# Shared feed-forward of an attention and mixture-of-experts block in pairs of half-precision numbers

## What is computed

```python
# x: (8, 256, 512), ctx: (8, 256, 512); 16 heads of 16 in 256 channels, 512 positions
q = Wq @ layernorm(x) + bq ; k = Wk @ ctx + bk ; v = Wv @ ctx + bv
x = x + masked_attention(q, k, v)
flat = layernorm(x).reshape(2048, 512)
shared_out = (sigmoid(flat @ shared_gate.T) * (flat @ shared_up.T)) @ shared_down.T     # 352 wide, float32
weights = softmax(flat @ router_w.T)                       # 8 experts, the best 2 of each row
routed = sum over the 2 experts of weight * expert(flat)   # bfloat16, 352 wide
out = x + shared_out + routed
```

## Time and profile before

| | |
|---|---|
| median of 3 runs | 753.3 us (752.68 to 756.65) |
| the profiled execution, its own time | 754.22 us |
| its span in the profile | 752.4 us |
| mean granted TensorE clock | 0.952 |
| PE / DVE / ACT / POOL busy | 87% / 66% / 59% / 38% of the span |
| attention on PE | 64 to 497 us |
| shared feed-forward, first half | 497 to 604 us |
| experts | 605 to 696 us |
| second half and stores | 696 to 752 us |

### The profile page before, as it was taken

One profiled execution on the slowest core, in us unless ns is written; L12 is line 12 of the kernel. 1 busy time (PEld: TensorE's weight loads), 2 busy tenths in 40 slices (PEclk: granted clock), 3 DMA queues, 4 the chain that ended last, 5 costly groups with the idle time before them and its releaser, 6 DMA issues.

```text
span 752.4 us, 11618 instructions
## 1 busy us (share of the span) xinstructions
PE 657.5 (87%) x3718; PEld 264.5 (35%) x3718; DVE 500.0 (66%) x984; ACT 445.7 (59%) x597; POOL 287.1 (38%) x420
## 2 busy tenths in 40 slices
PE   4589999999999999999999866778699989999984
PEld 3423323323323323323232211134344456665432
DVE  2487788888898898888888985202357035454647
ACT  3305878868778778778778768773530056665000
POOL 5623434633634554363544131313100244440664
PEclk9957999999999999999999986999899999999998
DMA  6433345354364463563433300428940023332445
GB/s 195 138 111 96 99 123 160 101 139 129 109 161 112 117 174 81 155 219 115 114 115 109 89 29 30 104 69 175 221 122 0 28 82 116 113 115 85 152 140 167
DMA packets 65610, 88.60 MB, mean 118 GB/s; under 512 B 12576, under 2 KB 46112, under 8 KB 64528
## 3 DMA queue, kind: packets, MB, share of 16 engines
q1 hardware_dynamic: 60992, 69.64, 31.1%
q0 software_dynamic: 4560, 18.22, 10.4%
HBM read 63.75 MB, written 32.74 MB: 128 GB/s over the span
## 4 chain that ended last, share of the span: by engine, by line
PE 69%; ACT 11%; DVE 8%; issue 5%; DMA 3%; another core or an unknown queue 1%; SPq 1%; POOL 0%; DVEq 0%; ACTq 0%; POOLq 0%
PE PS L752 15%; PE PS L919 10%; PE PS L724 10%; PE PS L659 8%; PE PS L533 7%; PE PS L1303 6%; ACT E L738 6%; PE PS L612 4%; PE PS L1365 3%; DVE MX L665 3%; PE PS L1152 2%; DVE ST L373 2%; ACT X L1168 1%; DVE X L1419 1%; PE PS L1270 1%
## 5 line engine op out<-in xcount | busy, mean ns | idle before, releaser
L665 DVE TENSOR_REDUCE MX<-PS 128x1 f32<-128x512 f32 x512 | 326.9, 684 | 65.0 <-PE PS L659 64.5
L738 ACT ACTIVATE E<-PS 128x1024 f32<-128x1024 f32 x256 | 258.9, 1020 | 77.0 <-PE PS L724 76.2
L752 PE MATMUL PS<-E,BIG 128*32 128x512 f32 x1024 | 141.9, 627 | 6.6 <-ACT E L738 6.6
L659 PE MATMUL PS<-BIG 53*128 53x512 f16 x512 | 123.1, 403 | 22.2 <-DVE MX L665 14.3
L724 PE MATMUL PS<-BIG 55*128 55x512 f16 x512 | 102.1, 397 | 27.3 <-ACT E L738 25.6
L567 POOL TENSOR_TENSOR ML<-BIG,ML 128x512 f32<-128x512 f32 x30 | 38.3, 1276 | 155.9 <-ACT BIG L543 155.9
L919 PE MATMUL PS<-E,SW 128*128 128x512 f32 (+2 forms) x192 | 85.7, 603 | 1.1 <-DVE ML L962 0.9
L724 PEld LDWEIGHTS PS<-BIG 55*128 55x128 f16 x512 | 24.5, 93 | 174.9 <-ACT E L738 106.3
L1254 POOL DMA_INDIRECT CT<-scr_yr,IX x39 | 37.0, 949 | 115.1 <-DVE IX L1112 54.8
L543 ACT ACTIVATE BIG<-PS,BIG 128x256 f32<-128x256 f32 x64 | 35.9, 564 | 49.2 <-PE PS L533 42.6
L1303 PE MATMUL PS<-BIG,CT 128*128 x312 | 53.0, 313 | 2.6 <-issue 2.6
(11 more groups left out here) (170 smaller groups left out, 773.0 us busy)
## 6 DMA issues: line engine op xcount, KB each, us to landing
scr_parts<-WP SPq DMA_DIRECT2D x96, 128.0 KB
BIG<-scr_parts SPq DMA_DIRECT2D x64, 192.0 KB
BIG<-in_we POOLq DMA_DIRECT2D x8, 1088.0 KB, 14.9
scr_u<-ML SPq DMA_DIRECT2D x32, 256.0 KB, 2.4
scr_ys<-XN SPq DMA_DIRECT2D x19, 256.0 KB
X<-in_x SPq DMA_DIRECT2D x8, 512.0 KB, 6.6
CT<-in_ctx SPq DMA_DIRECT2D x8, 512.0 KB, 6.2
ML<-scr_u SPq DMA_DIRECT2D x16, 256.0 KB
```

Of the source, the lines that this page charges most:

```text
L659: e.matmul(PS[:, yi[name] % 3, :], QK[rows, qb(u), 0, j0 + jj, 128 * tt:128 * tt + 128], QK[rows, qb(u), 1, j0 + jj, :], start=True, stop= ...
L665: e.tensor_reduce(MX[:, g % 2, c:c + 1], PS[:, yi[name] % 3, :], AX.X, ALU.max)\
L738: e.activation(E[:, st, 2 * jj:2 * jj + 2, :], PS[:, slot(name):slot(name) + 2, :], ACT.Exp, scale=1 / 1024).then_inc(s["rc"], 1)
L752: ins = e.matmul(PS[32 * hh:32 * hh + 32, AVB, :], VT[:, b % 2, st, 4 * (g % 4) + hh, :], E[:, st, hh, :], start=(st == 0), stop=(st == 3))
```

## The change

The shared weights are no longer kept as float32. For each of the three matrices (`m` = 0, 1, 2) `split_shared(m)` loads it to a staging tile (at 8.23, 9.23 and 10.23 in SP's queue), squares it on ACT with a running sum, sums over partitions by one matmul, takes the power -1/2 on POOL, scales the matrix there by it and splits it there into two float16 halves: high, and the rest (three POOL instructions on 128x1440, 128x1408 or 128x1536, at position 8.78, 9.78 or 10.78, after `balance` and ahead of the split of the keys). The activations are split likewise: ACT writes the high half, and DVE the rest, for the turned rows (`rest`, 128x1024) and for the hidden values (`upper` on ACT, `lower` on DVE, 128x512). Every float32 matmul of L919 and L1152 becomes three float16 ones (high by high, low by high, high by low). The scales are undone in the tanh, in the logits and in L1160. Norm 11 moves: its statistics from behind G(0, 0) to behind G(0, 2), its normalised rows from behind G(1, 2) to behind T(2, 0); the two last `add_base` move later.

```diff
-        def load_shared(e):
-            e.dma_start(SW[:, 0:1440], sg).then_inc(s["sw"], 16)
...
-        sp.at(10.02, load_shared)
...
+        for m in range(3):
+            mring.append((8 + m + 5.85 * IT, ("z", m)))
...
-                    if n > 8:
-                        e.wait_ge(s["ba"], n - 8)
-                    e.tensor_scalar(RR1[:, :], rr, 1.0, None, ALU.add)
+                    if n > 9:
+                        e.wait_ge(s["ba"], n - 9)
+                    e.tensor_scalar(RR1[:, n % 2, :], rr, 1.0, None, ALU.add)
...
+        def split_shared(m):
...
+            def load(e):
+                if m:
+                    e.wait_ge(s["sw"], m)
+                e.dma_start(part, (sg, su, sd)[m]).then_inc(s["sg"], 16)
+            sp.at(t0 - .5, load)
...
+                    ins = e.activation(junk, v, ACT.Square, accum_out=ZS[:, c0 + i:c0 + i + 1])
+                ins.then_inc(s["zq"], 1)
+            act.at(t0 - 1.2 * IT, squares)
...
+                e.matmul(PS[:, bank, 0:nc_], OO, ZS[:, c0:c0 + nc_], start=True, stop=True).then_inc(s["mp"], 1)
+            pe.at(t0, mm)
...
+            def factor(e):
+                e.wait_ge(s["mc"], yi[name] + 1)
+                z = ZC[:, c0:c0 + nc_]
+                pch.step(e, e.tensor_tensor(z, z, mhalf[:, 0:nc_], ALU.pow))
+                e.tensor_scalar(z, z, cells[0][2], None, ALU.mult).then_inc(s["zf"], 1)
+                e.wait_ge(s["zf"], m + 1)
...
+                    ins = e.tensor_tensor(v, v, f, ALU.mult)
+                pch.step(e, ins)
+                pch.step(e, e.tensor_tensor(out[:, 0:n], part, zero[:, 0:1].broadcast_to([128, n]), ALU.add))
+                e.tensor_tensor(out[:, n:2 * n], part, out[:, 0:n], ALU.subtract).then_inc(s["sw"], 1)
+            pool.at(t0 + .4 * IT, factor)
...
-                    e.wait_ge(s["h"], hq[p] + 1)
+                    e.wait_ge(s["hm"], hq[p] + 1)
...
-                e.activation(yT[blk][:, 2 * j:2 * j + 2, :], PS[:, pair:pair + 2, :], ACT.Copy).then_inc(s["te"], 1)
+                e.activation(yT[blk][:, 0, 2 * j:2 * j + 2, :], PS[:, pair:pair + 2, :], ACT.Copy).then_inc(s["y16"], 1)
             act.at(when(item) + .5 * dt_, evac)
+
+            def rest(e):
+                e.wait_ge(s["y16"], tq[item] + 1)
+                e.tensor_tensor(yT[blk][:, 1, 2 * j:2 * j + 2, :], PS[:, pair:pair + 2, :],
+                                yT[blk][:, 0, 2 * j:2 * j + 2, :], ALU.subtract).then_inc(s["te"], 1)
+            dve.at(when(item) + .6 * dt_, rest)
...
-                    ins = e.matmul(PS[0:wide, pair + c, :], (sgw, suw)[c][:, k, 128 * it:128 * it + wide],
-                                   yT[blk][:, k, :], start=(k == 0), stop=(k == 3))
+                    wt = (sgw, suw)[c]
+                    for a, r in ((0, 0), (0, 1), (1, 0)):
+                        ins = e.matmul(PS[0:wide, pair + c, :], wt[:, a, k, 128 * it:128 * it + wide],
+                                       yT[blk][:, r, k, :], start=(k == 0 and a == r == 0), stop=(k == 3 and a == 1))
...
+                e.scalar_tensor_tensor(full, full, 1.0, PS[0:w, pair + 1, :], ALU.add, ALU.mult).then_inc(s["hm"], 1)
+            dve.at(when(item) + .7 * dt_, hidden)
...
+                e.activation(dst[:, 0, :], full, ACT.Copy).then_inc(s["hi"], 1)
+            act.at(when(item) + .8 * dt_, upper)
+
+            def lower(e):
+                e.wait_ge(s["hi"], hq[item] + 1)
+                e.tensor_tensor(dst[:, 1, :], full, dst[:, 0, :], ALU.subtract).then_inc(s["h"], 1)
+            dve.at(when(item) + .92 * dt_, lower)
...
-                    ins = e.matmul(PS[:, bank, :], h, sdw[0:IW[it], it, :], start=(it == 0), stop=(it == 2))
+                    for a, c in ((0, 0), (0, 1), (1, 0)):
+                        ins = e.matmul(PS[:, bank, :], h[:, a, n], sdw[0:IW[it], c, it, :],
+                                       start=(it == a == c == 0), stop=(it == 2 and a == 1))
...
-        norm(11, t0 + .8 * dt_, t0 + .85 * dt_, when(("G", 1, 2)) + .56 * dt_)
+        norm(11, when(("G", 0, 2)) + .94 * dt_, when(("G", 0, 2)) + .95 * dt_, when(("T", 2, 0)) + .62 * dt_)
...
-        act.at(when(("T", 0, 1)) + .61 * dt_, add_base(2))
-        act.at(when(("G", 1, 2)) + .57 * dt_, add_base(3))
+        act.at(when(("G", 1, 2)) + .85 * dt_, add_base(2))
+        act.at(when(("R", 2)) + .85 * dt_, add_base(3))
```

More of the change, by code:

```diff
@@ L140, in xattn_moe, with pair16 @@
         ZP = ef[:, 1664:1760].bitcast(HF).rearrange("p (r k t) -> p r k t", r=2, k=3)
-        yT = [E[:, b, :, :] for b in range(4)]
+        yT = [E[:, b, :, :].rearrange("p k t -> p (k t)").bitcast(HF).rearrange("p (r k t) -> p r k t", r=2, k=4)
+              for b in range(4)]
+        def pair16(v):
+            return v.bitcast(HF).rearrange("p (r t) -> p r t", r=2)
         TH = WP[:, 2048:3072].rearrange("p (a n) -> p a n", a=2)
@@ L821, in xattn_moe @@
             balance(b)
+        for m in range(3):
+            split_shared(m)
         norm(0, -12, -13, -11)
@@ L932, in tanh @@
                         e.wait_ge(s["dn"], dq["R", blk - 1] + 1)
-                    e.activation(LG, PS[96:104, pair, :], ACT.Copy).then_inc(s["lg"], 1)
+                    e.activation(LG, PS[96:104, pair, :], ACT.Identity, scale=ZI[96:104, 1:2]).then_inc(s["lg"], 1)
                 if hq[item] >= 2:
@@ L938, in tanh, with upper @@
                     e.wait_ge(s_pw[1], 48 * NU)
-                e.activation(TH[0:w, hq[item] % 2, :], PS[0:w, pair, :], ACT.Tanh, scale=0.5).then_inc(s["th"], 1)
+                e.activation(TH[0:w, hq[item] % 2, :], PS[0:w, pair, :], ACT.Tanh, scale=ZI[0:w, 0:1]).then_inc(s["th"], 1)
             act.at(when(item) + .5 * dt_, tanh)
+            if it == 2:
+                dst = pair16(HS2[0:w, H2[blk], :])
+            elif blk >= 2:
+                dst = pair16(E[0:w, 1, 2 * (blk - 2) + it, :])
+            else:
+                dst = pair16(HS[0:w, blk, it, :])
+            full = TH[0:w, hq[item] % 2, :]
             def hidden(e):
                 e.wait_ge(s["th"], hq[item] + 1)
+                e.scalar_tensor_tensor(full, full, 1.0, PS[0:w, pair + 1, :], ALU.add, ALU.mult).then_inc(s["hm"], 1)
+            dve.at(when(item) + .7 * dt_, hidden)
+            def upper(e):
+                e.wait_ge(s["hm"], hq[item] + 1)
                 if it == 2:
-                    e.wait_ge(s["lg"], blk + 1)
                     if blk == 0:
@@ L950, in hidden @@
                         e.wait_ge(s["a"], NU - 1 if blk == 1 else NU)
[L951 to L964 removed]
+                elif blk >= 2:
+                    e.wait_ge(s["hm"], hq[item])
+                else:
+                    e.wait_ge(s["rp"], NRING)
+                    e.wait_ge(s["mp"], NMX)
+                    e.wait_ge(s_pw[0], 48 * NU)
+                e.activation(dst[:, 0, :], full, ACT.Copy).then_inc(s["hi"], 1)
[4 more added lines that the diff above has]
+            dve.at(when(item) + .92 * dt_, lower)
         def router(blk):
@@ L1159, in evac @@
                 acc = X[:, 4 * blk + nt, :]
-                e.scalar_tensor_tensor(acc, PS[:, bank, :], 0.5, acc, ALU.mult, ALU.add).then_inc(s["de"], 1)
+                e.scalar_tensor_tensor(acc, PS[:, bank, :], ZO, acc, ALU.mult, ALU.add).then_inc(s["de"], 1)
             dve.at(when(item) + .7 * dt_, evac)
@@ L1167, in f @@
                     x = X[:, 4 * blk + nt, :]
-                    ins = e.activation(x, x, ACT.Identity, bias=NMR[:, blk % 2, nt:nt + 1], scale=RR1[:, nt:nt + 1])
+                    ins = e.activation(x, x, ACT.Identity, bias=NMR[:, blk % 2, nt:nt + 1], scale=RR1[:, blk % 2, nt:nt + 1])
                 ins.then_inc(s["ba"], 1)
@@ L1233, in f @@
                     e.wait_ge(s["rc"], zi["k", 15, 1] + 1)
+                    e.wait_ge(s["sw"], 3)
                 if i >= 5:
```

75 lines of the change are left out of this document (54 added, 21 removed), and 2 rows, old and new, of the table s.

## The result

The changed kernel takes 772.4 us, median of 4 runs (769.85 to 774.75), beside 753.25 for the kernel before on the same chip: ratio 1.024, 95% interval 1.0195 to 1.0292. It is slower by 19 us. 765 was forecast, with a range up to 776. The profiled execution took 774.75, with a span of 773.0 us and a mean granted clock of 0.917 (before 0.952).

What follows compares the result with a forecast made beforehand. PE was taken to bound attention, with 3 to 4 us of slack on the side path. 754.2 + 23 - 4.5 - 6.5 = 766.2 profiled, 0.9 lower for the median: 765 us; forecast 757 to 773, 8-in-10 range 748 to 776.

Steps and rivals of the forecast that it cites:

- attention at +23: Attention's summed loss: 11.0 weight split, 6.0 loads, less 0.8 for old loads, 4.2 clock, 2.5 squares.
- Part 3: Second half of the feed-forward: POOL's gathers bound it, so PE's gain is limited; -6.5 us, bounds -8.8 and 0.
- POOL's split: Attention: splitting three weight matrices on POOL delays the key split and the maxima's placing, stalling PE 11.0 us together.
- The rest is delay: Attention: POOL work beyond its idle time delays the key split by 7.4, 6.9 and 7.9 us.
- leave no start-up cost to save: Attention: POOL's 3.47 us per 512 elements was taken to scale with length, giving some 11 us per matrix.
- The loads ahead of the placing: Attention: the second and third weight load hold up the maxima's small DMA, 3.0 us each; 6.0, bounds 0 and 6.5.
- The squares: Attention: squaring the weights on ACT, with three matmuls with ones, costs 2.5 us, bounds 0 and 6.
- The clock: Attention: three stalls of PE each bring a slower clock behind them, 1.4 us each; 4.2, bounds 0 and 9.
- Part 2: First half of the feed-forward: nothing gained before counting, 6 us from there, of which -4.5 kept; bounds -9 and +1.
- case of late results that recur: Second half: if DVE again gets its results late, its last eight tiles start at 731 as before and nothing is gained.
- The split stays hidden: Faster rival: POOL's work under some 7 us per matrix stays covered, attention loses only +3; 745 us, chance 0.14.
- The stalls spread: Slower rival: cold starts cost 3 each, first half gains nothing, late results recur in the second; 778 us, chance 0.13.

Runs made afterwards that it cites:

- experiment 1: The changed kernel with the three weight loads issued just behind the placing of the maxima, not just ahead of it; 763.9 us, ratio 1.018.
- experiment 3: The changed kernel with the edits of experiment 2 and experiment 1 together; 769.9 us, ratio 1.022.
- experiment 4: experiment 3 with the loads moved further ahead and the squares on ACT moved away from those of `balance`; 757.3 us, ratio 1.005.
- experiment 9: experiment 6 with the first block's router steps on DVE and the two last `add_base` on ACT moved; 752.9 us, ratio 0.996.
- experiments 9 to 12: experiment 9, experiment 10, the kernel before with the router and `add_base(3)` moves of experiment 9 (753.5 us, ratio 0.9995), and experiment 12.
- experiment 8: The changed kernel with norm 11 and the two last `add_base` back at their old places; 777.4 us, ratio 1.032.
- experiment 12: experiment 10 run once more, unchanged; 751.8 us, ratio 0.993 to the kernel before.
- experiment 7: The changed kernel with two of the three products per tile left out in the second half of the feed-forward; 764.6 us, ratio 1.018.
- experiment 5: experiment 4 with each of POOL's three large steps on a weight matrix cut into four instructions; 754.3 us, ratio 1.009.
- experiment 6: experiment 5 with POOL's scaling and narrowing right behind the power and only the subtraction behind the residual's add; 752.3 us, ratio 1.001.
- experiment 2: The changed kernel with POOL's three large steps moved behind the key split, and a second staging tile; 765.0 us, ratio 1.017.
- experiment 10: experiment 9 with the first `rest` on DVE put ahead of attention's last reciprocal; 749.1 us, ratio 0.991.

## Why the prediction was right, and where it wasn't

**The outcome** was forecast, slower by 12 with 19 measured, inside the range but near its upper end, and attention at +23 is close to the measured +20.9. The parts of that sum were less good than the sum.

That the sum came out near is partly luck: waits for the placing were put at 11.0 + 6.0 and took 8.35, while waits behind DVE (+3.5) and 1.9 us lost before half unit 14 were not in it, and the clock took 2.7 more. In Part 3 nothing of the gain came.

**POOL's split: +11.0 was forecast, and with the loads out of the way it brings no wait for the placing.** The step that failed is the one from POOL's work to delay, "The rest is delay", and then from delay to stall. The three steps of POOL took 2.53 to 3.13 us each on 1408 to 1536 elements where 512 take 1.04 to 1.28: from 512 to 1408 the narrowing grows by 1.49 us in 896 elements, 1.66 ns each, so some 0.19 of each narrowing is start-up (an estimate from these two lengths). The prediction had said that these rows "leave no start-up cost to save". So the key split was late by 5.6, 4.4 and 4.4 us against the rest of attention, and not by 7.4, 6.9 and 7.9. With the loads out of the way no wait for the placing was left (experiment 1), and at half unit 23 of the changed kernel neither.

It may not have been nothing in the changed kernel itself: at half unit 19 of the changed kernel PE was ready at 319.89, and the placing's second DMA without the load ahead would have been issued at 319.6 and landed 1.8 later, 1.5 us late. That is an estimate; in experiment 1 PE had lost 1.67 us to DVE by then, and the placing was in time.

**The loads ahead of the placing: +6.0 was forecast, and they decide whether the split shows.** Together with the split they cost 8.35 us of waits, and 4.57 and 2.64 in two other profiles of the same attention; with one of the two out of the way 0 to 1.2 is left. That both are needed is why adding one term to another was wrong: the first eats the slack of 3 to 4 us, the second then counts. The row that the 6.0 was read from shows less than the prediction took from it: the last old load had landed at 339.34, 4.1 us before PE's late start at 343.41, so it alone doesn't explain that wait. The waits behind the new loads do show it.

**The squares: 2.5 was forecast, 4.5 measured** in experiment 3 (6.5 us at three starts that waited 2.0 in the kernel before), inside the bounds of 0 and 6; moving them took 2.7 off (experiment 4). ACT has gaps, but PE waits for the exponential next in its queue, and the squares stood right behind those of `balance`. In the changed kernel two of these three waits hid behind the ones for the placing.

**What POOL's new steps do to DVE** was a term that was missing. Between 285 and 400 PE's waits behind DVE rose from 0.5 to 4.0 us in the changed kernel, and up to 5.5 in experiment 4; with POOL's steps cut in four they were 2.3.

**The clock: 4.2 was forecast, 6.9 measured** in the profile, inside the bounds of 0 and 9, and 10 to 15 in two other executions of the same attention. Over these three profiles it spreads by 8 us and the waits by 3, so it has the larger part in what one execution differs from another.

**Part 2: -4.5 was forecast, -3.5 measured** (109.2 to 105.8). The parts fit: no gain up to counting, as carried on (+1.5 for 0), and -5.0 for -6 behind it. The start of G(0, 2) came 8.2 us behind attention's last copy for 4.0, 4.2 later where 3.6 stood. The chain was right to name `rest`, `add_base(2)` and the router's steps as what the items wait for; experiment 9 took 9 us out of just these places. The experts' +1.6 was not forecast: the clock was low for 3.4 us at their start.

**Part 3: -6.5 was forecast, +1.5 measured.** The last stage was over 54 us, the mark that the prediction set for a refutation. Its case of late results that recur, nothing gained, is what happened. They don't come with one kernel: all six profiles of three occasions have them (before, changed, experiments 9 to 12: 52.6 to 54.4 us), none of the eight of the two others (44.5 to 45.9), and the same last stage stands in both groups (the changed kernel and experiment 8). Whether the occasion decides or the single execution stays open: three of the twelve runs of experiment 12 took 744.4 to 744.7 us and the others 749.1 or more, a gap that the late results would explain, but no profile of a short one exists. Nor does one of the kernel before without late results, so whether the change gains anything there when they are absent stays open too. Its medians give no sign of the 8 us: 753.1 and 750.3 on the occasions without, 753.3, 756.2 and 754.2 on the others. That PE isn't the bound is shown (experiment 7).

**The rivals.** "The split stays hidden" had the mechanism, and its threshold was too low: it asked for less than 7 us of POOL's work on a matrix, and with the loads behind the placing more than 9 leave no wait for it. It failed on the loads. "The stalls spread" fell on the first half, which did gain. The changed kernel is slower because of where it puts steps that have room elsewhere: with them moved, POOL's steps cut in four and nothing left out it is 0.7 to 0.9% faster than before.

## What to carry to other kernels

A side path with 3 to 4 us of slack takes one new step and not two, so new steps are costed together and not one by one; what stands ahead of a small urgent DMA counts with its bytes. When the matmuls of a stage get shorter (an item of 7.1 us became one of 5.35), the queues of the other engines become its schedule: look again at every step that stands between two of PE's inputs. And compare stages, not totals: two kernels with the same attention differed by 8 us there (experiments 7 and 8), more than either edit was worth.

## What the runs showed of the hardware that was not expected

A long POOL instruction holds up short DVE ones: multiplies of 0.19 us with both inputs in SBUF took up to 3.08, and in the changed kernel itself a scaling of 0.18 us (L752, one input) took 1.89 beside L575 of POOL. Four instructions for one shorten it: in experiment 5 the multiply took 0.49 at most and the scaling 0.85. The price is some 0.14 us of POOL for each instruction more (2.96 us for four narrowings of 352 elements in experiment 6, 2.53 for one of 1408).

The clock's cost comes with the waits but not in proportion: 13.5 us of waits went with 3.5 us of clock loss in experiment 2 and 13.6 with 9.2 in experiment 3. In the changed kernel the lower level was granted for 6.8 us around the end of each of the two waits of 4 us (323.1 to 329.9 and 357.2 to 364.0).

By the profile, PE's results can reach DVE in the last stage many us behind the matmuls' ends, and then several at once, in some profiles and not in others. In experiment 10 DVE stood for 9.46 us while PE, by its records, had three tiles ready:

```profile
725.47 0.75 DVE L1273 SCALAR_TENSOR_TENSOR X<-PS,TB,X 128x512 f32<-128x512 f32 x1 [9.46 <-remote]
726.32 1.61 DVE L1533 SCALAR_TENSOR_TENSOR X<-E,M,X 128x512 f32<-128x512 bf16 x2
```

In that time PE's own matmuls came one by one, 1.4 us apart, for some 4 us (717.02 to 721.23), with nothing named that they waited for. Whether the matmuls or only their signals were late, and what causes it, was not tried.
